# Reordering SyncE's transfers in a recurrence step: half copies, with small-packet key copies between them

## What is computed

```python
xn = _layernorm(x, axis=-1)
x = x + _L0_gnn_ref(xn, ...) + _L0_mix_ref(xn[None], ...)[0]
x = x + _L0_ffn_ref(_layernorm(x, axis=-1)[None], ...)[0]
...
def step(S, x):
    qt, kt, vt, bt, gt = x
    S = S * jnp.exp(gt)[..., None, None]
    kv = jnp.einsum('bhk,ebhkv->ebhv', kt, S)
    delta = (vt[None] - kv) * bt[..., None]
    S = S + kt[None, :, :, :, None] * delta[..., None, :]
    ot = jnp.einsum('bhk,ebhkv->ebhv', qt * scale, S)
    return (S, ot)
```

## Time and profile before

| | |
|---|---|
| median of 3 runs | 900.23 us (900.04 to 902.91) |
| the profiled execution | 899.98 us |
| its span (first to last instruction) | 897.7 us |
| PE busy (matmul) | 818.5 us, 91% |
| DVE / ACT / POOL busy | 618.5 / 311.9 / 338.8 us |
| q1 (all that SP issues) | 69733 packets, 57.78 MB, 23.0% of 16 DMA engines |
| q8 (instruction blocks) | 84 packets, 1.38 MB, 0.6% |
| chain that ended last | PE 67%, DVE 23%, issue 4% |

### The profile page before, as it was taken

One profiled execution on the slowest core, in us unless ns is written; L12 is line 12 of the kernel. 1 busy time (PEld: TensorE's weight loads), 2 busy tenths in 40 slices (PEclk: granted clock), 3 DMA queues, 4 the chain that ended last, 5 costly groups with the idle time before them and its releaser, 6 DMA issues.

```text
span 897.7 us, 24280 instructions
## 1 busy us (share of the span) xinstructions
PE 818.5 (91%) x10394; PEld 552.7 (62%) x10394; DVE 618.5 (69%) x1306; ACT 311.9 (35%) x548; POOL 338.8 (38%) x300
## 2 busy tenths in 40 slices
PE   2999999999999989998999978998899989997898
PEld 1454444445566548763444357888889989897443
DVE  7999999976888556328633647766667757673385
ACT  1231112210222120023545525454545555554352
POOL 5221100000111040001760358776677776762560
PEclk9999999999999989999899989999999999999999
DMA  8500000030000042000085744454534444421462
GB/s 247 183 0 1 0 2 1 17 76 23 2 1 2 2 171 87 1 1 0 6 309 199 264 129 115 115 138 117 137 114 139 123 132 123 130 70 44 111 187 68
DMA packets 74961, 80.49 MB, mean 90 GB/s; under 512 B 34452, under 2 KB 57670, under 8 KB 74853
## 3 DMA queue, kind: packets, MB, share of 16 engines
q1 hardware_dynamic: 69733, 57.78, 23.0%
q0 software_dynamic: 5120, 21.14, 6.6%
HBM read 54.44 MB, written 24.39 MB: 88 GB/s over the span
## 4 chain that ended last, share of the span: by engine, by line
PE 67%; DVE 23%; issue 4%; DMA 2%; ACT 2%; POOL 1%; SPq 1%; DVEq 0%; POOLq 0%
PE bank L772 10%; PE bank L841 10%; PE bank L867 5%; PE bank L1042 4%; PE bank L582 4%; DVE rows L1541 4%; PE bank L568 4%; DVE rows L1543 3%; PE bank L788 3%; DVE rows L1670 3%; PE bank L930 2%; PE bank L789 2%; PE bank L858 2%; PE bank L943 2%; PE bank L967 2%
## 5 line engine op out<-in xcount | busy, mean ns | idle before, releaser
L772 PE MATMUL bank<-W,xT 128*128 128x512 f32 x272 | 123.8, 608 | 4.8 <-ACT big L1119 4.8
L772 PEld LDWEIGHTS bank<-W,xT 128*128 128x128 f32 x272 | 51.6, 194 | 64.5 <-issue 57.9
L546 PE MATMUL bank<-W,xT 128*125 128x512 f32 x160 | 77.8, 600 | 0.0
L1361 POOL TENSOR_TENSOR cnt_r<-cnt_r,ident_sb 125x125 fp32r<-125x125 f32 x10 | 11.4, 1142 | 173.8 <-ACT cnt_r L1107 173.8
L568 PEld LDWEIGHTS bank<-rows 128*126 128x126 f16 x360 | 43.5, 135 | 34.7 <-issue 24.2
L1676 DVE TENSOR_SCALAR rows<-iota_sb,tC 128x625 f16<-128x625 f16 x180 | 56.2, 379 | 10.5 <-PE bank L568 10.5
L568 PE MATMUL bank<-rows 128*126 128x313 f16 x360 | 58.9, 299 | 4.2 <-DVE rows L1676 4.1
L1541 DVE TENSOR_SCALAR rows<-iota_sb,gbp 125x180 f16<-125x180 f16 x160 | 56.8, 355 | 0.0
L1543 DVE TENSOR_SCALAR rows<-iota_sb,gbp 125x180 f16<-125x180 f16 x160 | 51.0, 318 | 0.0
L841 PE MATMUL bank<-big 64*64 64x64 f32 (+1 forms) x1280 | 44.3, 214 | 4.0 <-issue 3.2
L556 PE MATMUL bank<-rows 125*128 125x360 f16 x160 | 42.5, 319 | 5.1 <-DVE rows L1543 3.5
(11 more groups left out here) (337 smaller groups left out, 1975.8 us busy)
## 6 DMA issues: line engine op xcount, KB each, us to landing
big<-qkv_slots SPq DMA_DIRECT2D x40, 256.0 KB, 3.6
rows<-step_rows SPq DMA_DIRECT2D x40, 128.0 KB, 3.2
rows<-gam_rows SPq DMA_DIRECT2D x40, 128.0 KB, 3.4
big<-qkv_slots SPq DMA_DIRECT2D x80, 64.0 KB, 2.9
big<-qkv_slots SPq DMA_DIRECT2D x40, 128.0 KB, 2.9
o_slots<-big SPq DMA_DIRECT2D x40, 128.0 KB, 2.9
x_all<-in_x SPq DMA_DIRECT2D x10, 224.0 KB
out<-tC SPq DMA_DIRECT2D x10, 224.0 KB
```

Of the source, the lines that this page charges most:

```text
L546: last = mm(dst, xT[:, k, t * P:(t + 1) * P], W[:, w, k, :], start=(k == 0), stop=(k == KC - 1 and bias is None))
L772: last = mm(bank[:, b0, :], xT[:, k, t * P:t * P + 128], W[:, w, k, :], start=(k == 0), stop=(k == KC - 1))
```

## The change

The same 14 transfers per step are issued in another order, and three of the waits are gone (`t_psum`, `s_psum`, `uu_psum`). `load_rows`, `load_kp`, `load_vp` and `store_o` take an argument `halves`, so that each half can be issued by itself.

```diff
             for h in range(NSC + 3):
-                if h + 2 < NSC:
+                ahead, keys = h + 2 < NSC, h + 1 < NSC
+                if ahead:
                     sp.wait_ge(S["eb_done"], h + 1)
                     sp.wait_ge(S["kk_psum"], h + 1)
-                    load_rows(arow[h % 2], step_rows, h + 2, arow_loaded[h % 2])
+                    load_rows(arow[h % 2], step_rows, h + 2, arow_loaded[h % 2], (0,))
+                if 1 <= h and keys:
+                    sp.wait_ge(S["kd_done"], h)
+                load_kp(h + 1, 0, (0,))
+                if ahead:
+                    load_rows(arow[h % 2], step_rows, h + 2, arow_loaded[h % 2], (1,))
+                load_kp(h + 1, 0, (1,))
+                if ahead:
                     sp.wait_ge(S["feat_psum"], h + 1)
-                    if h >= 1:
-                        sp.wait_ge(S["t_psum"], h)
                     load_qk(h + 2, 1)
                 if h >= 3:
-                    store_o(h - 3)
-                if h + 2 < NSC:
+                    store_o(h - 3, (0,))
+                load_kp(h + 1, 1, (0,))
+                if h >= 3:
+                    store_o(h - 3, (1,))
+                load_kp(h + 1, 1, (1,))
+                if ahead:
                     sp.wait_ge(S["m_psum"], level_count(h, 1))
                     load_qk(h + 2, 0)
-                if 1 <= h < NSC - 1:
-                    sp.wait_ge(S["kd_done"], h)
-                if 2 <= h < NSC - 1:
-                    sp.wait_ge(S["s_psum"], 2 * h - 3)
-                load_kp(h + 1, 0)
-                if 1 <= h < NSC - 1:
-                    sp.wait_ge(S["uu_psum"], h)
-                load_kp(h + 1, 1)
+                    sp.wait_ge(S["qg_done"], h + 1)
+                    load_rows(grow[h % 2], gam_rows, h + 2, grow_loaded[h % 2], (0,))
+                if 2 <= h < NSC:
+                    sp.wait_ge(S["y_ready"], 2 * h - 2)
                 if h < NSC:
-                    if h >= 2:
-                        sp.wait_ge(S["y_ready"], 2 * h - 2)
-                    load_vp(h)
-                if h + 2 < NSC:
-                    sp.wait_ge(S["qg_done"], h + 1)
-                    load_rows(grow[h % 2], gam_rows, h + 2, grow_loaded[h % 2])
+                    load_vp(h, (0,))
+                if ahead:
+                    load_rows(grow[h % 2], gam_rows, h + 2, grow_loaded[h % 2], (1,))
+                if h < NSC:
+                    load_vp(h, (1,))
```

More of the change, by code:

```diff
@@ L449, in _, with load_rows, load_kp, load_vp @@
             sp.wait_ge(S["slot_rows_written"], 16 * 9 + 64)
-            def load_rows(dst, rws, u, loaded):
+            def load_rows(dst, rws, u, loaded, halves=(0, 1)):
                 per = rws.rearrange("(u c b j) n -> u b c (j n)", c=2, b=2, j=HB)
-                for b in range(2):
+                for b in halves:
                     sp.dma_start(dst[CL * b:CL * b + CL, :, :].rearrange("p (c j) n -> p c (j n)", c=2),
                                  per[u, b].partition_broadcast(CL)).then_inc(loaded, 16)
-            def load_kp(u, c):
+            def load_kp(u, c, halves=(0, 1)):
                 per = qkv_slots[0:PSLOTS, D:2 * D].rearrange("(u c p) (j b n) -> u b p c j n", c=2, p=CL, b=2, n=DH)
                 if u < NSC:
-                    for b in range(2):
+                    for b in halves:
                         sp.dma_start(kp[u % 2][CL * b:CL * b + CL, c * HB:(c + 1) * HB, :], per[u, b][:, c]).then_inc(kp_loaded[u % 2], 16)
-            def load_vp(u):
+            def load_vp(u, halves=(0, 1)):
                 per = qkv_slots[0:PSLOTS, 2 * D:3 * D].rearrange("(u c p) (b n) -> u b p c n", c=2, p=CL, b=2)
-                for b in range(2):
+                for b in halves:
                     sp.dma_start(vp[u % 2][CL * b:CL * b + CL, :, :].rearrange("p (c j) n -> p c (j n)", c=2),
@@ L470, in load_qk, with store_o @@
                 sp.dma_start(qkn[u % 2][:, w * D:(w + 1) * D], qkv_slots[u * SCH:(u + 1) * SCH, w * D:(w + 1) * D]).then_inc(qk_loaded[u % 2], 16)
-            def store_o(u):
+            def store_o(u, halves=(0, 1)):
                 sp.wait_ge(S["o_done"], 2 * u + 2)
                 per = o_slots[0:PSLOTS, :].rearrange("(u c p) (b n) -> u b p c n", c=2, p=CL, b=2)
-                for b in range(2):
+                for b in halves:
                     sp.dma_start(per[u, b], ot[u % 2][CL * b:CL * b + CL, :, :]).then_inc(o_stored[u % 2], 16)
```

## The result

The changed kernel takes 910.4 us (median of 6 runs, 905.97 to 913.74) against 900.32 us for the kernel before, measured beside it (6 runs, 896.71 to 902.94). The ratio is 1.0106, with a 95% interval of 1.0069 to 1.0143: slower by about 1%. The profiled execution took 910.51 us, its span is 908.3 us.

The account below looks back on a forecast made before the run. PE was taken to bound the recurrence, stalling for instruction blocks held behind full DMA stretches. Terms -7 + 1 = -6 us against the profiled 899.98 gave 894.0, and 894.2 us as median; range 885 to 906.

Parts of the forecast that it names:

- What bounds the kernel: Recurrence, 534 to 790 us: PE bounds it, loads are on time, 25 us are real stalls for TensorE's instruction blocks.
- That nothing else would move: SP's issues in a recurrence step: all end by T + 9.2, not T + 12.5; moved waits and instructions cost 0.
- The rival with a wait in front of the queue: Half the decay rows behind kd_done at the step's head: GpSimd late delays the step, 918 us; chance 0.05, unforeseen causes included.
- the term of +1 us: Recurrence steps: price of key copies in the decay rows' stretch and of shorter breaks, taken as 1 us between 0 and 9.
- full stretch: About 3 us per step with DMA engines full (keys, outputs, queries, 768 KB); instruction blocks falling in it come late.
- The halving, the term of -7 us: Full stretches broken by key copies into runs of 1.5 us: late blocks wait half as long, gaining 7 us.
- The size of the pool: Recurrence stalls: 12 blocks fall in full stretches at 1.13 us each, about 14 of the 25 us.
- The part of that term for the mixed stretch: Head of the step, key copies among decay rows: within the 1 us price, bounded by 0 and 9 us.
- The rival "slower by density": From T + 2.5 to T + 7.5, two runs close into one of 5 us: +9 us, 909 us; chance 0.17.

Follow-up runs that it names:

- sixteen_partitions: The kernel before, with every load of a recurrence step cut to 16 partitions from unit 2 on, output stores whole; ratio 0.9939.
- keycopies_in_outputs: The kernel before, with the second pair of key copies placed between and behind the output halves, the uu_psum wait left in front of the values; ratio 1.0088.
- both shifted pairs: Old and new order with 128 or 64 PE instructions added ahead of the recurrence; ratios to before 1.0001 and 1.0075 (128), 1.0056 and 1.0148 (64).
- keycopies_in_first_rows: The kernel before, with the first pair of key copies placed between the halves of the first decay rows, all else as before; ratio 1.0047.
- queries_late: The kernel before, with the queries and the second pair of key copies moved behind the values, ahead of the second decay rows; ratio 1.0032.

## Why the prediction was wrong

**What bounds the kernel** was right: PE, with no engine waiting for the loads, and stalls that are for the most part waits for instruction blocks and grow with what SP has in flight. The landings of the blocks show the first half of that, sixteen_partitions the second by experiment.

**That nothing else would move** held: SP's timeline is the one worked out, to within 1.3 us at the end; `kd_done`, `o_done` and `qg_done` cost SP next to nothing (2.3 us for the last in 17 steps). PE's waits for DVE, which I had not counted on, grew by 1.4 us. The rival with a wait in front of the queue did not occur.

**The step that failed** is the price of what the change puts between the full stretches, the term of +1 us for "the key copies in the decay rows' stretch" and "the shorter breaks", and under it the premise that only a full stretch holds blocks up. I had taken one block that came at the end of a full stretch and made a rule of it. The change fills the third quarter of the step from 0.22 to 0.62 of the DMA engines' time, and the border stalls whose block starts there grew from 8.2 to 16.8 us; those of the first and fourth quarter grew by 3 more. No window there has to be full for that. keycopies_in_outputs, one of the edits that were to help, lost 0.9%, with 15.9 us in the third quarter.

**The halving, the term of -7 us**, is the smaller miss. "each run of big pieces ends at a key copy of 64 KB, which ... lets the DMA engines catch up" did not come out as a lower load: the second quarter stayed at 0.73. Its full windows did become fewer, and the stalls of the blocks that start in it fell from 11.7 to 6.9 us, 4.8 where I had 7. They fell in both shifted pairs too. All four quarters together give -4.8 + 8.6 + 3.2 = +7 us over this stretch, where the forecast had -6. These are single executions; the direction is the same in three pairs, the sizes are not.

**The size of the pool** was nearly right: I gave 14 of the 25 us to blocks in full stretches, and 11.7 of the 21.7 us at borders are those of the second quarter. By the Trainium skill (Runtime: NRT & Kernel Launch, Instruction fetch mechanics) crossing a block border is mostly hidden. The trace does not agree for this code: 21.7 us in 256 are stalls at borders.

**The part of that term for the mixed stretch**, decay rows and key copies at the head of the step, measured 0.0047, about 4 us, in keycopies_in_first_rows, between its bounds of 0 and 9. It was chosen by the share of the windows, and the share is a poor measure.

**The rival "slower by density"** gave 909 us, and the median is 910.4; it had 0.17. Its price came out, its mechanism only in part. It said that two stretches would close into one full one of 5 us; what came is a dense one that is nowhere full for long. And density is not the only measure: queries_late spreads the same load more evenly by quarters and loses 0.3%. What exactly makes one order of the same bytes better than another for the instruction blocks stays open. The traces give a part of it. From PE's passing of one border to the start of the transfer of the block for the next, there are 2.3 us on average before, 2.6 in the changed kernel and 1.5 in sixteen_partitions, over the same 52 blocks; the transfer itself takes 1.1 us in all three. So what grows is the time before a block's transfer starts. When PE asks for it these profiles do not hold.

## What to carry to other kernels

When the bounding engine stalls for its own instructions, the order of other transfers matters even though nobody waits for them; count these stalls in a run with most of the data cut away, since a new order will win little of what is left there, and count only those at block borders. Do not judge a schedule of DMAs by its fullest microsecond: here the stalls behind the fullest stretch got fewer, those behind the medium load that was spread into the breaks doubled, and the kernel got slower. A change of 0.5% in such a kernel can come from instructions that do no work, so compare two orders at two or three shifts of the code before believing either.

## What the runs showed of the hardware that was not expected

- 64 PE instructions that are executed in idle time, ahead of the recurrence, made the kernel slower by 0.0056 (0.0031 to 0.0082); 128 of them changed nothing (1.0001).
- Three waits at which SP stood idle were worth 0.75%: taking away a wait on a queue that is not on the path made the kernel slower.
- TensorE stood 21.7 us in 256 for its own instructions before, and 7.0 with the DMA engines at 0.20 of their time. Each of these stalls over 0.2 us ended 1.2 to 1.6 us after the block of that place had landed.
